# Causal attention inside a transformer block: where the masks are applied, how key tiles are paired, and how row sums are inverted

## Chip, cores and metric

One core of a Trainium2 chip runs the whole kernel in one launch. The metric is the device time of that launch in microseconds. Lower is better.

## What is computed

One adaLN transformer block in float32 on x of shape (2, 2048, 512): two sequences of 2048 tokens, width 512, 16 heads of 32. Cut to what matters here:

```python
mod = silu(condition) @ Wada + bada
sh_a, sc_a, gt_a, sh_m, sc_m, gt_m = split(mod, 6)
xm = layernorm(x, g1, be1) * (1 + sc_a) + sh_a
q, k, v = split(xm @ Wqkv)                      # 16 heads of 32
scores = where(causal, q @ k.T * 32 ** -0.5, -inf)
x = x + gt_a * (softmax(scores) @ v @ Wproj + bproj)
xm = layernorm(x, g2, be2) * (1 + sc_m) + sh_m
x = x + gt_m * (gelu(xm @ W1 + b1) @ W2 + b2)
```

## The kernel before

The program has four phases, one after the other: qkv, attention, projection, MLP. The change is in `phase_attention`, which runs 8 groups (2 sequences x 4 bundles of GH = 4 heads). `Plan` (a class that fixes the order of work for one group) cuts a group's causal triangle into 40 steps. A step is one key tile of 128 keys against one query chunk of 512 queries, for 4 heads. The chunks are taken from the last to the first (positions pos 0 to 3), with 16, 12, 8 and 4 key tiles. In the last four steps of each position the tile crosses the diagonal, and only the queries from `mid` on are computed: widths 512, 384, 256 and 128.

The softmax needs the maximum of every query row first. So there are two streams of work on TensorE:

* **The maxima of the next chunk** (`item`, tile `mx`, three PSUM banks). One item is a 128-query x up to 512-key tile of scores (L887), reduced along its row by VectorE (`tensor_reduce`, L800). A group has 160 such tiles (64 for pos 0, 48, 32, 16) and four small transposes of the collected maxima (`turn`, L879, L813, L815). 64 of the 160 tiles lie on the diagonal, in equal numbers of widths 128, 256, 384 and 512. TensorE may write a bank again only when VectorE has reduced the tile three items earlier (semaphore `mx_free`). `Plan.items_at` spreads the 164 items over the steps.
* **The steps themselves.** `scores` writes four tiles `st`, one per head (L907; the maximum is subtracted inside the matmul through two extra rows). ScalarE takes `Exp` of each into `prob` (L759). `product` multiplies the probabilities by v into `o_ps` (L925): four heads on four column groups of 32, which the trace shows as a run of 8. The row sums come by one of two ways: **direct**, a second run of ones x prob into `r_ps` (L930), or **pooled**, where GpSimd adds the whole `prob` tile of 2048 columns into `psum_k` (L740) and one run of ones x psum_k at the end (`total`, L942) adds it in.

The order on TensorE is written out by hand in `body`: scores of step s, then the product of step s - 1, with the items put between heads (`between`), between the product and the row sums, and behind them (`Plan.place`).

Causal masks are added on TensorE before: an extra matmul of a bfloat16 identity with a triangle of -1e30, into the last 128 columns of each diagonal tile (L890 for `mx`, L910 for `st`).

At the end of a position ScalarE copies `o_ps` and `r_ps` to SBUF (L768, L770), VectorE inverts the row sums in four pieces of 128 columns (`invert`, L824) and multiplies (`finish`, L830). SP stores `o_sb`. SP also sends the maxima through DRAM into the two extra rows of `q_st`.

## Time and profile before

| | |
|---|---|
| runs | 2533.92 us median of 3 (2533.89 to 2537.0) |
| profiled execution, first to last instruction (span) | 2531.2 us |
| around the span, against the median run | 2.7 us |
| busy in the span | PE 2367.6, PEld 1522.2, DVE 1370.5, ACT 907.9, POOL 731.3 us |
| attention, from the first product to the last | 391.6 to 1624.8 us |

The profile shows one execution. PE is TensorE's matmuls, PEld its weight loads, DVE VectorE, ACT ScalarE, POOL GpSimd, SP SyncE. A busy PE is no proof of a full PE, since matmuls are pipelined and a record is longer than the distance to the next one. Distances between starts are therefore read from the timeline where an engine's rate matters.

### The profile page before, as it was taken

The page shows a single profiled execution, that of the slowest core. Times are in us where ns is not written, and L with a number is a line of the kernel's source. Part 1 is how long each engine was busy: PE and PEld are TensorE (multiplying, and loading weights), DVE is VectorE, ACT ScalarE, POOL GpSimd, SP SyncE. Part 2 cuts the span into 40 slices and gives each one's busy share as a digit, 9 for nine tenths or more (in the row PEclk, how much of TensorE's full clock was granted, in tenths as well). Part 3 has the DMA queues.
Part 4 walks back from the last instruction along what each step waited for, and adds up shares of the span by engine and source line. Part 5 has one row for each costly group of instructions (what it writes and reads, how often), then busy time and mean ns, then how long its engine had stood idle before and what let it go on. Part 6 is the DMA issues. An engine that isn't in the chain of part 4 may idle for free. (4 is left out here: it accounts for less than half of the span.)

```text
span 2531.2 us, 38127 instructions
## 1 busy us (share of the span) xinstructions
PE 2367.6 (94%) x12615; PEld 1522.2 (60%) x12615; DVE 1370.5 (54%) x2406; ACT 907.9 (36%) x1772; POOL 731.3 (29%) x239
## 2 busy tenths in 40 slices
PE   6999958999999999999999999789599999999998
PEld 5888834444444444444444444467488888888887
DVE  6566455677777776776777773256622221221222
ACT  2111104454545545555454544311332222222221
POOL 1000025545554554555535554265000000000000
PEclk9999958999999999999999998789799999999999
DMA  5444464242242432515243211247521101110100
GB/s 183 167 182 174 158 158 102 55 96 63 64 98 56 105 69 53 109 40 125 49 91 79 60 35 47 87 176 244 171 84 50 50 1 49 50 50 0 50 33 17
DMA packets 129055, 223.34 MB, mean 88 GB/s; under 512 B 8448, under 2 KB 25912, under 8 KB 128828
## 3 DMA queue, kind: packets, MB, share of 16 engines
q1 hardware_dynamic: 105660, 175.18, 25.9%
q10 hardware_dynamic: 23232, 46.14, 5.0%
q8 instruction: 84, 1.38, 0.2%
q14 instruction: 79, 0.65, 0.1%
HBM read 145.26 MB, written 76.02 MB: 87 GB/s over the span
## 5 line engine op out<-in xcount | busy, mean ns | idle before, releaser
L800 DVE TENSOR_REDUCE part<-mx 128x1 f32<-128x512 f32 (+1 forms) x1249 | 690.2, 600 | 245.0 <-PE mx L890 127.8
L759 ACT ACTIVATE prob<-st 128x512 f32<-128x512 f32 (+3 forms) x1280 | 600.7, 538 | 579.0 <-PE st L907 357.7
L740 POOL TENSOR_TENSOR psum_k<-psum_k,prob 128x2048 f32<-128x2048 f32 (+3 forms) x136 | 519.0, 3817 | 242.3 <-ACT prob L759 238.4
L887 PE MATMUL mx<-k_st,qx_st 96*128 96x512 f32 (+1 forms) x1249 | 494.3, 422 | 41.2 <-DMA k_st<-qk_scratch 21.7
L907 PE MATMUL st<-q_st,k_st 98*128 98x512 f32 (+3 forms) x1280 | 471.4, 416 | 27.5 <-DMA q_st<-m_scratch 8.8
L887 PEld LDWEIGHTS mx<-k_st,qx_st 96*128 96x128 f32 x1249 | 241.3, 197 | 272.8 <-DVE part L800 223.9
L1442 DVE TENSOR_TENSOR m_g_lo<-m_g,m_g_hi 128x512 fp32r<-128x512 f32 x128 | 88.6, 692 | 511.8 <-ACT m_g_hi L1406 511.8
L907 PEld LDWEIGHTS st<-q_st,k_st 98*128 98x128 f32 x1280 | 243.0, 196 | 178.4 <-ACT prob L759 84.0
L925 PE MATMUL o_ps<-prob,v_sb 128*32 128x512 f32 (+3 forms) x2560 | 310.3, 557 | 0.0
L1402 ACT ACTIVATE m_g<-m_hid,vcol 128x512 f32<-128x512 f32 x128 | 88.3, 690 | 494.8 <-PE m_hid L1534 494.7
L740 POOL TENSOR_TENSOR psum_k<-prob 128x2048 f32<-128x2048 f32 x24 | 109.4, 4560 | 395.0 <-ACT prob L759 395.0
L1534 PE MATMUL m_hid<-m_xm_hi,w_hi 128*128 128x512 f32 x512 | 200.8, 392 | 16.3 <-DVEq L1471 10.4
L824 DVE RECIPROCAL o_raw<-o_raw 128x128 f32<-128x128 f32 x128 | 114.2, 926 | 166.5 <-ACT o_raw L770 165.2
L1534 PE MATMUL m_hid<-m_xm_hi,w_lo 128*128 128x512 f32 x512 | 199.7, 390 | 0.0
L1534 PE MATMUL m_hid<-m_xm_lo,w_hi 128*128 128x512 f32 x512 | 199.7, 390 | 0.0
L1512 PE MATMUL m_acc<-w_hi,m_g_hi 128*128 128x512 f32 x512 | 199.2, 389 | 0.0
L1512 PE MATMUL m_acc<-w_hi,m_g_lo 128*128 128x512 f32 x512 | 199.2, 389 | 0.0
L1512 PE MATMUL m_acc<-w_lo,m_g_hi 128*128 128x512 f32 x512 | 199.2, 389 | 0.0
L930 PE MATMUL r_ps<-prob,ones 128*32 128x512 f32 (+3 forms) x1088 | 125.1, 532 | 0.0
L1534 PEld LDWEIGHTS m_hid<-m_xm_hi,w_hi 128*128 128x128 f32 x512 | 96.5, 188 | 39.8 <-issue 19.9
L890 PE MATMUL mx<-mask_qk,ident_bf 128*128 128x128 bf16 x505 | 117.4, 236 | 0.0
L910 PE MATMUL st<-mask_kq,ident_bf 128*128 128x128 bf16 x512 | 116.9, 233 | 0.0
(160 smaller groups left out, 2667.7 us busy)
## 6 DMA issues: line engine op xcount, KB each, us to landing
qx_st<-qk_scratch SPq DMA_DIRECT2D x96, 256.0 KB, 4.5
k_st<-qk_scratch SPq DMA_DIRECT2D x96, 256.0 KB, 8.2
q_st<-qk_scratch SPq DMA_DIRECT2D x96, 256.0 KB
qk_scratch<-st_hi ACTq DMA_DIRECT2D x16, 1024.0 KB, 4.2
qk_scratch<-st_lo ACTq DMA_DIRECT2D x16, 1024.0 KB, 6.4
xs<-in_x_dram SPq DMA_DIRECT2D x8, 1024.0 KB, 5.3
v_scratch<-st_v ACTq DMA_DIRECT2D x8, 1024.0 KB, 4.3
v_sb<-v_scratch SPq DMA_DIRECT2D x8, 1024.0 KB, 14.6
```

The source lines that it names most:

```text
L740: nc.gpsimd.tensor_tensor(dst, src, prob[:, s % BUF, :, m:], ALU.add).then_inc(pool_added, 1)
L759: nc.scalar.activation(prob[:, s % BUF, h, m:], st[n % RING][:, m:], ACT.Exp, scale=SCALE).then_inc(exp_done, 1)
L800: nc.vector.tensor_reduce(part[:, pos % 2, h * TT + t, kc:kc + 1], bank[:, 0:w], AX.X, ALU.max).then_inc(mx_free, 1)
L824: nc.vector.reciprocal(r, r).then_inc(inverted, 1)
L887: ins = nc.tensor.matmul(out[:, 0:w], qx_st[0:ROWS, pos % 2, h, t * P:(t + 1) * P], k_st[0:ROWS, u, h, kc * CH:kc * CH + w], start=True, s ...
L890: ins = nc.tensor.matmul(out[:, w - P:w], K.ident_bf[:, :], K.mask_qk[:, :], start=False, stop=True)
L907: ins = nc.tensor.matmul(out[:, m:], k_st[0:MROWS, u, h, kt * P:(kt + 1) * P], q_st[0:MROWS, pos % 2, h, m:], start=True, stop=not masked)
L910: ins = nc.tensor.matmul(out[:, m:m + P], K.ident_bf[:, :], K.mask_kq[:, :], start=False, stop=True)
L925: ins = nc.tensor.matmul(o_ps[rows, m:], v_sb[:, u, kt, rows], prob[:, s % BUF, h, m:], start=(kt == 0), stop=end)
L930: ins = nc.tensor.matmul(r_ps[h * HD:(h + 1) * HD, m:], K.ones[:, 0:HD], prob[:, s % BUF, h, m:], start=(kt == 0), stop=end and pos == QC - 1)
L1512: ins = nc.tensor.matmul(acc[s][:, :], a, b, start=(j == 0 and k == 0), stop=(j == HT - 1 and k == 2))
L1534: ins = nc.tensor.matmul(hid[j % 4][:, :], a, b, start=(t == 0 and k == 0), stop=(t == KT - 1 and k == 2))
```

## The change

* **Masks.** The masking matmuls are gone. For the maxima, a diagonal tile is reduced by `tensor_tensor_reduce` on VectorE, which adds a mask row of 512 bfloat16 columns and takes the maximum. For the probabilities, GpSimd sets the triangle of 4 x 128 columns of each of the 16 diagonal steps of a group to zero after Exp (`affine_select`), and the product and the adds wait for it (`masked`).
* **Pairs.** Scores of two steps run one after the other, then the products of the two steps before, with nothing between. Items stand between the heads of the scores alone. `prob` has 5 buffers in place of 4.
* **Row sums.** A table `POOLED` says which key tiles GpSimd adds: 11, 8, 4 and 0 of the 16, 12, 8 and 4. That leaves 5, 4, 4 and 4 direct steps, 17 as before, of which 13 are diagonal ones. GpSimd has 20 adds a group, as before, now all of full width. `total` follows at once on the last product of a position.
* **Inversion.** VectorE transposes `r_ps` in 32 x 32 blocks, inverts 16 columns, transposes them back spread over 512, and multiplies. ScalarE's copy of `r_ps` is gone.
* The weights by which `Plan` spreads the items change, and `gate` is allocated after attention.

```diff
-    DIRECT = 3
+    POOLED = {3: (0, 1, 2, 4, 5, 6, 7, 9, 10, 11, 12), 2: (0, 1, 2, 4, 5, 6, 7, 8), 1: (0, 1, 2, 4), 0: ()}
...
-        weight = [self.width(s) + (P if self.steps[s][0] == 0 else 0) for s in range(self.NS)]
-        FROM, TO = 2, self.NS - 5
+        weight = [GH * max(self.width(s) / 2.4 + 13, 200) + 1.7 * self.width(s) for s in range(self.NS)]
+        FROM, TO = 2, self.NS - 6
...
-    BUF = 4
+    BUF = 5
...
+            def select(g, s):
+                n, m = L.selects.index(s), L.mid(s)
+                await_count(pool, held_pool, exp_done, exp_count(g, GH * (s + 1)))
+                tri = prob[:, s % BUF, :, m:m + P]
+                nc.gpsimd.affine_select(out=tri, in_=tri, compare_op=ALU.is_ge, fill=0.0, base=0,
+                                        pattern=[[0, GH], [1, P]], channel_multiplier=-1).then_inc(masked, 1)
...
             def body(g, u, more):
+                for s in range(L.NS):
+                    if s in L.selects:
+                        select(g, s)
+                    if s - 1 in L.adds:
+                        add(g, s - 1)
...
-                nc.scalar.activation(o_raw[:, pos % 2, 1, :], r_ps[:, :], ACT.Copy).then_inc(o_copied, 1)
...
-                dve.wait_ge(mx_ready, pre + 1)
-                nc.vector.tensor_reduce(part[:, pos % 2, h * TT + t, kc:kc + 1], bank[:, 0:w], AX.X, ALU.max).then_inc(mx_free, 1)
+                most = part[:, pos % 2, h * TT + t, kc:kc + 1]
+                if kc == L.order[pos]:
+                    await_count(dve, held_dve, mx_ready, pre + 1)
+                    nc.vector.tensor_tensor_reduce(spare[:, 0:w], bank[:, 0:w], K.mask_row[:, CH - w:], 1.0, LOWEST,
+                                                   ALU.add, ALU.max, most).then_inc(mx_free, 1)
+                else:
+                    dve.wait_ge(mx_ready, pre + 1)
+                    nc.vector.tensor_reduce(most, bank[:, 0:w], AX.X, ALU.max).then_inc(mx_free, 1)
...
-                nc.vector.reciprocal(r, r).then_inc(inverted, 1)
...
+            def normal(g, pos, part):
+                n = QC * g + pos
+                if part == 0:
+                    dve.wait_ge(r_ready, r_count(g, pos + 1))
+                    nc.vector.transpose(r_turn[:, :, :].rearrange("p b i -> p (b i)"), r_ps[:, :]).then_inc(r_taken, 1)
+                elif part == 1:
+                    dve.wait_ge(r_taken, n + 2)
+                    nc.vector.reciprocal(r_inv[:, :, :], r_turn[:, :, 0:1]).then_inc(r_inverted, 1)
...
+                elif part == 3:
+                    dve.wait_ge(r_spread, n + 1)
+                    dve.wait_ge(o_copied, n + 2)
+                    dve.wait_ge(o_sb_free, n + 1)
+                    nc.vector.tensor_tensor(o_sb[:, pos % 2, :], o_raw[:, pos % 2, :], r_wide[:, :],
+                                            ALU.mult).then_inc(o_done, 1)
...
-                if diagonal:
-                    ins = nc.tensor.matmul(out[:, w - P:w], K.ident_bf[:, :], K.mask_qk[:, :], start=False, stop=True)
...
-                    if masked:
-                        ins = nc.tensor.matmul(out[:, m:m + P], K.ident_bf[:, :], K.mask_kq[:, :], start=False, stop=True)
...
                 pe.wait_ge(exp_done, exp_count(g, GH * (s + 1)))
+                if L.diagonal(s):
+                    pe.wait_ge(masked, mask_count(g, L.selects.index(s) + 1))
...
-                    if s < L.NS:
-                        scores(g, u, s, between)
-                    elif more:
-                        scores(g + 1, 1 - u, 0)
-                    product(g, u, s - 1, between)
+                for b in range(1, L.NB + 1):
+                    for s in (2 * b, 2 * b + 1):
...
+                        if s < L.NS:
+                            scores(g, u, s, between)
+                        elif more:
+                            scores(g + 1, 1 - u, s - L.NS)
+                    for s in (2 * b - 2, 2 * b - 1):
+                        product(g, u, s)
```

How the order on the engines moves is shown at three places.

TensorE before, position 0, the products of steps 6 and 7. `mx` is a tile for the maxima, `st` a tile of scores, `o_ps` the product run, `r_ps` the row-sum run.

```order
837 L925 MATMUL o_ps<-prob,v_sb 32x512 x4
838 L876 REGISTER_ALU
839 L887 MATMUL mx<-k_st,qx_st 128x512
840 L930 MATMUL r_ps<-prob,ones 32x512 x4
841 L876 REGISTER_ALU
842 L887 MATMUL mx<-k_st,qx_st 128x512
843 L905 REGISTER_ALU
844 L907 MATMUL st<-q_st,k_st 128x512
```

TensorE of the change, the same position: the scores with their items end, then comes the product run of two steps (x8 is two runs of four), then the next scores.

```order
822 L938 MATMUL st<-q_st,k_st 128x512
823 L913 REGISTER_ALU
824 L923 MATMUL mx<-k_st,qx_st 128x512
825 L955 MATMUL o_ps<-prob,v_sb 32x512 x8
826 L937 REGISTER_ALU
827 L938 MATMUL st<-q_st,k_st 128x512
828 L913 REGISTER_ALU
829 L923 MATMUL mx<-k_st,qx_st 128x512
```

The `mx` matmuls that stood beside each product are between the scores now. Nothing that VectorE could reduce is issued while a product run lasts.

VectorE of the change, in position 1, where position 0's row sums are inverted. A diagonal tile is two instructions, both at L828: the one that writes `unused`, and one that writes `part`.

```order
493 L857 STREAM_TRANSPOSE r_turn<-r_ps 128x512
494 L51 REGISTER_ALU
495 L828 ISA unused,part<-mx,mask_row 128x512
496 L828 ISA part 128x1
497 L860 RECIPROCAL r_inv<-r_turn 128x16
498 L51 REGISTER_ALU
499 L828 ISA unused,part<-mx,mask_row 128x128
500 L828 ISA part 128x1
501 L863 STREAM_TRANSPOSE r_wide<-r_inv 128x512
502 L51 REGISTER_ALU
503 L828 ISA unused,part<-mx,mask_row 128x256
504 L828 ISA part 128x1
```

One part of the inversion is put in front of each reduction. Before, four reciprocals of 128 columns stood there, one in each of four steps.

## Rows read from the trace of the kernel before

**Rows 1.** Busy time by engine (PE, PEld, DVE, ACT, POOL), clock, DMA: attention alone.
```profile
391.60:1624.80 1233.20, 1186.60 (x7480) 572.65 (x7479) 843.08 (x1464) 627.96 (x1336) 628.48 (x160) 0.97 0.32 72
```

**Rows 2.** Waits between 420 and 1600 us: total, times, longest.
```profile
PEld mx L887 <- DVE part L800: 210.4, 297, 1.6
```

**Rows 3.** Timeline of PE: start us, us, op, count, idle before.
```profile
866.67 0.47 PE L887 MATMUL mx<-k_st,qx_st 96*128 96x512 f32 x1
866.99 0.23 PE L890 MATMUL mx<-mask_qk,ident_bf 128*128 128x128 bf16 x1
867.03 0.48 PE L907 MATMUL st<-q_st,k_st 98*128 98x512 f32 x1
...
868.54 0.40 PE L887 MATMUL mx<-k_st,qx_st 96*128 96x512 f32 x1
868.87 1.06 PE L925 MATMUL o_ps<-prob,v_sb 128*32 128x512 f32 x8
869.86 0.50 PE L887 MATMUL mx<-k_st,qx_st 96*128 96x512 f32 x1
870.29 1.06 PE L930 MATMUL r_ps<-prob,ones 128*32 128x512 f32 x8
871.29 0.50 PE L887 MATMUL mx<-k_st,qx_st 96*128 96x512 f32 x1
871.62 0.40 PE L907 MATMUL st<-q_st,k_st 98*128 98x512 f32 x1
871.86 0.40 PE L887 MATMUL mx<-k_st,qx_st 96*128 96x512 f32 x1
```

**Rows 4.** Timeline of PE where two runs follow each other directly.
```profile
994.34 1.07 PE L925 MATMUL o_ps<-prob,v_sb 128*32 128x512 f32 x8
995.22 1.04 PE L930 MATMUL r_ps<-prob,ones 128*32 128x512 f32 x8
996.19 0.38 PE L907 MATMUL st<-q_st,k_st 98*128 98x256 f32 x1
```

**Rows 5.** Groups by line and shape: busy us, mean ns; then idle before.
```profile
L890 PE MATMUL mx<-mask_qk,ident_bf 128*128 128x128 bf16 x505 | 117.4, 236 | 0.0
L910 PE MATMUL st<-mask_kq,ident_bf 128*128 128x128 bf16 x512 | 116.9, 233 | 0.0
```

**Rows 6.** Groups by line and shape: VectorE's reductions, reciprocals and one tiny operation.
```profile
L800 DVE TENSOR_REDUCE part<-mx 128x1 f32<-128x512 f32 x869 | 552.8, 681 | 162.0 <-PE mx L887 106.9 <-PE mx L890 51.1 <-DVE m_lo L815 1.7
L824 DVE RECIPROCAL o_raw<-o_raw 128x128 f32<-128x128 f32 x128 | 114.2, 926 | 166.5 <-ACT o_raw L770 165.2 <-DVE m_lo L815 1.1
...
L800 DVE TENSOR_REDUCE part<-mx 128x1 f32<-128x128 f32 x127 | 34.9, 275 | 53.2 <-PE mx L890 53.2
...
L99 DVE TENSOR_SCALAR tmp<-tmp 128x4 f32<-128x4 f32 x8 | 1.4, 169 | 0.3
```

**Rows 7.** Timeline of DVE: two full-width reductions in a row.
```profile
903.26 1.29 DVE L800 TENSOR_REDUCE part<-mx 128x1 f32<-128x512 f32 x2 [0.20 <-PE mx L887]
```

**Rows 8.** Timeline of POOL and DVE: the multiply that closes a position.
```profile
936.66 4.57 POOL L740 TENSOR_TENSOR psum_k<-psum_k,prob 128x2048 f32<-128x2048 f32 x1 [5.06 <-ACT prob L759]
...
939.52 2.26 DVE L830 TENSOR_TENSOR o_sb<-o_raw 128x512 f32<-128x512 f32 x1
```

**Rows 9.** Groups by line and shape: GpSimd's adds and a select.
```profile
L740 POOL TENSOR_TENSOR psum_k<-psum_k,prob 128x2048 f32<-128x2048 f32 x88 | 403.2, 4582 | 182.8 <-ACT prob L759 180.3
...
L209 POOL TENSOR_SCALAR_AFFINE_SELECT ident_bf<-ident_bf 128x128 bf16<-128x128 bf16 x1 | 0.3, 293 | 0.0
```

**Rows 10.** Timeline of the projection phase: DVE reads PSUM and SBUF while POOL adds.
```profile
1780.13 4.99 POOL L1109 TENSOR_TENSOR p_xs<-p_gated,p_xs 128x512 f32<-128x512 f32 x4 [11.14 <-DVE p_gated L1191]
...
1782.79 0.69 DVE L1191 TENSOR_TENSOR p_gated<-p_acc,gate 128x512 f32<-128x512 f32 x1 [1.61 <-PE p_acc L1254]
```

**Rows 11.** Timeline of PE at the start of a group.
```profile
1007.22 2.01 PE L907 MATMUL st<-q_st,k_st 98*128 98x512 f32 x4 [3.92 <-issue]
1009.16 1.93 PE L925 MATMUL o_ps<-prob,v_sb 128*32 128x512 f32 x8
```

More of the change, by code:

```diff
@@ L480, in direct, with first_direct, diagonal @@
         pos, kt = self.steps[s]
-        return pos == QC - 1 or kt % self.DIRECT == 0
+        return kt not in self.POOLED[self.order[pos]]
+    def first_direct(self, s):
+        pos, _ = self.steps[s]
+        return self.direct(s) and not any(self.direct(r) for r in range(s) if self.steps[r][0] == pos)
+    def diagonal(self, s):
+        pos, kt = self.steps[s]
+        return kt >= self.order[pos] * TT
     def mid(self, s):
@@ L500, in stream, with own_until @@
         return [i for i in self.items_at[s] if more or self.group(0, i) == 0]
+    def own_until(self):
+        return max(s for s in range(self.NS) if self.stream(s, False))
     def group(self, g, i):
@@ L520, in phase_attention @@
     ROWS, MROWS = 3 * HD, 3 * HD + 2
-    BUF = 4
+    BUF = 5
     RING = 3
-    INV = 4
+    SQ = 32
     M0, M1 = M_GTA, M_GTM + KT
-    MOD_AT, LOAD_AT = (25, 28, 34, 37), (28, 31)
     EACH = 6
+    first = L.own_until() + 1
+    MOD_AT = tuple(first + 3 * n for n in range(4))
+    LOAD_AT = (MOD_AT[0] + 3, MOD_AT[1] + 3)
     MROW = GH * TT
@@ new lines, in body @@
+            def body(g, u, more):
+                for b in range(1, L.NB + 1):
+                    items = L.stream(2 * b, more) + L.stream(2 * b + 1, more)
+                    ending = [p for p in range(QC - 1) if L.last_block[p] + 2 == b]
+                    for k in range(max(len(items), 6 if ending else 0)):
+                        if ending and k >= 2:
+                            normal(g, ending[0], k - 2)
+                        if k < len(items):
+                            i = items[k]
+                            item(L.group(g, i), item_count(g, i), L.items[i], mx[i % RING], unused[:, i % RING, :])
+                for k in range(4):
+                    normal(g, QC - 1, k)
@@ L927, in product, with total @@
                 if L.direct(s):
-                    between(GH)
+                    opens = L.first_direct(s)
+                    if opens:
+                        pe.wait_ge(r_taken, QC * g + pos + 1)
                     for h in range(GH):
                         ins = nc.tensor.matmul(r_ps[h * HD:(h + 1) * HD, m:], K.ones[:, 0:HD], prob[:, s % BUF, h, m:],
-                                               start=(kt == 0), stop=end and pos == QC - 1)
+                                               start=opens, stop=end and pos == QC - 1)
                 ins.then_inc(pv_done, 1)
-                between(GH + 1 if L.direct(s) else GH)
-                if end and pos == QC - 1:
+                if end:
+                    total(g, s, pos)
+            def total(g, s, pos):
+                if pos == QC - 1:
                     pe.wait_ge(pv_done, pv_count(g, s + 1))
-                    pe.sem_inc(o_ready, 1)
-            def total(g, pos):
-                n = sum(s <= L.last[pos] for s in L.adds)
+                    pe.sem_inc(r_ready, 1)
+                    return
+                n = sum(r <= s for r in L.adds)
                 pe.wait_ge(pool_added, add_count(g, n))
```

188 lines of the change are left out of this document (88 added, 100 removed).

## Prediction

> **What bounds the kernel now.** I first read the busy times of attention alone, from the first product to the last: 1233.2 us for 8 groups, so 154 us a group [rows 1]. PE is busy 1186.6 us of it, DVE 843.1, ACT 628.0 and POOL 628.5. The reader should see that PE is the bound and that DVE, the next one, has 68% of its time filled. The phases before and after attention are not touched, so the whole change is decided here. Then I read the waits: PEld waits 210.4 us, 297 times, for DVE to reduce a tile (`mx_free`) [rows 2]. These waits are short (1.6 us at most) and mostly lie under a running matmul, but they say that VectorE's three banks are the second limit, close behind. The timeline of PE gives the rates: two full-width plain matmuls start 0.24 us apart (871.62 to 871.86), while a record is 0.40 long [rows 3]. DVE starts full-width reductions 0.61 us apart (1.29 less the 0.68 of the second) [rows 6, 7]. So one tile and the `st` beside it cost PE 0.48 us and DVE 0.61 us. Where items crowd, DVE is the slower of the two.
>
> **The change on TensorE.** *Masks.* With its mask a full tile takes 0.36 us to the next start (866.67 to 867.03), without 0.24: 0.12 saved [rows 3]. The lower bound is 0.04, the distance from the mask to the next start. There are 1017 masks, 127 a group [rows 5]: 5 to 15 us a group. *Pairs.* Entering a run costs 0.33 in place of 0.24 (868.54 to 868.87), leaving it 0.99 in place of 0.88 where the next run follows directly, and the matmul behind takes 0.33 in place of 0.24 (871.29 to 871.62) [rows 3, 4]. That is 0.3 us for each time PE changes over. A group has 40 product runs and some 9 row-sum runs that stand apart; 20 pairs remain: 29 x 0.3 = 9 us. *Row sums.* The direct steps of a group have 7168 columns now and 5632 after, 3 runs of 512 less: 3 x 0.88 = 3 us. Together TensorE sheds 17 to 27 us of 154.
>
> **VectorE.** Four positions x four reciprocals x 0.86 us go (0.93 busy, less an overlap of 0.07 as in the reductions) [rows 6]: 14 us a group. What comes: two transposes of 512 columns, taken as 0.6 us each like a reduction, and a reciprocal of 16 columns, 0.2: 6 us in four positions. And 64 tiles become masked reductions of two instructions. The first I take like a plain reduction of its width. The second is not in this trace. Its bounds are nothing and 0.17 us, the duration of an operation on 128x4 [rows 6]; I take 0.10, nearer to that row since it has to follow its partner: 6 us. So VectorE's work hardly falls, 14 less against 12 more.
>
> **What the pairing does to VectorE is the step on which all turns.** Before, tiles stood beside and between the runs, so DVE always had something to reduce. Now it gets none during two to four runs (1.9 to 3.6 us), only the three tiles in the banks. For a pair with n items the stretch of scores lasts the longer of
>
> * PE: (8 + n) x 0.24
> * DVE: 0.9 + (n - 3) x d, since item n can be issued when item n - 3 is reduced; 0.9 is the way from the first score to the first reduction and from the last release to the last matmul (two plain starts and a matmul's record of 0.40).
>
> d is the mean distance of reductions: 0.61 at 512, 0.20 at 128 (0.275 less the same overlap), on the mean of a group's 96 full and 64 diagonal tiles 0.525 plus 0.4 x 0.10 = 0.565 [rows 6, 7]. The plan of the changed kernel gives the pairs 15, 9, 9, 10, 12, 11, 6, 11, 14, 14, 11, 8, 6, 9, 10, 8, 1, 0, 0, 0 items. From nine on DVE is the longer term, for 12 of the 20. Summed: 7.7 + 2 x 7.1 + 6.0 + 3 x 5.4 + 2 x 4.9 + 3 x 4.3 + 2 x 3.8 + 2 x 3.4, and some 10 for the four pairs without tiles: 91 us. The runs: 19456 product columns are 38 x 0.88, row sums 11 x 0.88, three totals 2.6, 20 changes of 0.3: 52 us. The four transposes of maxima, each with a chain of small operations on DVE, cost about 1 us each: 4. The wait that PE shows at the start of every second group (3.92 us, and a product run of 1.93 us behind it in place of 1.06) stays [rows 11]: 2 to 3.
>
> *The multiply.* One more wait grows. The multiply that closes a position took 2.26 us where GpSimd was adding and ended 0.55 us after that add did; undisturbed it would be as long as other passes of 512 columns, 0.69 [rows 8, 10]. It reads two tiles in SBUF. GpSimd's adds grow from 78 us a group to 20 x 4.58 = 92, plus 16 selects [rows 9], in a shorter or equal time, so the multiply meets an add in most positions and waits half of it, 2.3 us. Three of four positions have tiles queued behind it on DVE, and PE behind those. With the transposes (1.5 us) and 0.6 for itself: some 4 us each, 12 in a group.
>
> Sum of a group: 91 + 52 + 4 + 2.5 + 12 = 161.5 against 154: **7 us more**, in 7 groups 49. The last group has no tiles of a following one after half its steps, so it is bound by PE there and keeps about half of what PE sheds, 10 us. The opening 16 diagonal tiles add 2. I round the sum of +41 down to +36, since of the waits counted here some fall together. The profiled execution's 2531 becomes 2567; the median of the runs is 2.7 us above its span, so **2570 us**.
>
> The page "VectorE: DVE Perf Modes" of the Trainium skill, section "The TRN2 errata — SBUF-src ops pay a fixed extra latency per instruction", gives a PSUM-to-SBUF operation 120 cycles plus its columns at 0.96 GHz. At 512 columns that is an estimate of 0.66 us, where the trace's reductions start 0.61 apart; by the page's rate the crowded pairs would be some 5 us a group longer still, about 2610 us. The measured distance decides.
>
> *Selects on GpSimd.* One select on 128 columns took 0.29 us [rows 9]; on 4 x 128, between 0.3 and four of them, 1.2 us. Sixteen make at most 19 us a group, with the adds 111 of 160. The product waits for the select, but a pair later, some 6 us after Exp. That covers one add of 4.58 and a select. I cost it at nothing; without the cover it is the rival below. ScalarE loses a copy and bounds nothing.
>
> **The rivals.**
>
> 1. *The masked reductions and the multiply are cheap, and PE's gain comes through* (faster). If the second instruction is free, d is 0.525, and 99 crowded intervals give back 4 us; if the multiply seldom meets an add, 7 more. A group is then 150.5, and the time is 2534 - 25 - 10, about 2500. It decides where d plus the closing work falls below what PE sheds. For it: TensorE's saving is certain, and half of the multiplies of before were undisturbed. Against it: GpSimd's adds fill more of the group. Chance 0.24.
> 2. *Both sides cancel* within 5 us: 0.08.
> 3. *GpSimd is late with a select* (slower). It is in order, so the first diagonal steps of a position have their selects behind adds of 4.58 us. If each of two such places in a group lets PE wait for a whole add, that is 9 us a group on top, 2640. It decides if a select takes 2 us or more. Chance 0.09.
> 4. *The masked reduction meets GpSimd's adds as the multiply does*, since its mask row is in SBUF. Each of 64 tiles would wait 0.6 x 2.3 us, some 90 us a group, over 3200 us. The trace speaks against it: a pass that read one tile in PSUM and one in SBUF took 0.69 us in the middle of four adds of GpSimd [rows 10]. Chance 0.02.
> 5. *The clock.* PE's idle pieces grow. After the 3.92 us of idleness a product run took 1.93 us in place of 1.06 [rows 11], which is the lower of the two clock levels. If longer waits in crowded pairs bring that back, each costs a few us. Chance 0.02, beyond 2600.
> 6. My forecast, VectorE's rate in crowded pairs, slower by 10 to 75 us: 0.55; its own range is 2545 to 2610.
>
> **How the numbers follow.** About 0.2% (5 us) is what a measurement of this kernel can tell from no change. Faster is rival 1, 0.24; same is rival 2, 0.08; slower the rest, 0.68. The range leaves out the fast end of rival 1 (below 2505) and rivals 4 and 5: 2505 to 2635.
>
> **What would show it.** In the changed profile: PE's busy time in attention falls by over 100 us while the span of attention does not; waits of PE for DVE's reductions grow to several times 210 us and are longest in the pairs with 14 and 15 items; DVE idles in the product runs; the multiply lasts over 2 us on the mean; no wait on a select shows. The forecast is wrong if PE's waits for DVE stay near 200 us, if the accumulator's instruction is free, or if PE waits for GpSimd.

## The result, and the profile after

| | before | after |
|---|---|---|
| runs | 2533.9 us median of 4 (2528.32 to 2537.0) | 2592.22 us median of 4 (2584.19 to 2600.81) |
| profiled execution, span | 2531.2 us | 2599.1 us |
| attention, first to last product | 1233.2 us | 1297.5 us |
| one group, mean of the first seven | 153.1 us | 162.9 us |
| mean granted TensorE clock over the whole span | 0.961 | 0.910 |

The change makes the kernel slower: after / before is 1.0237, interval 1.0205 to 1.0269, which is 60 us. In the profiled executions attention accounts for 64 us of a difference of 68. The first product starts 7 us later (398.5 against 391.6), and what follows attention is 3 us shorter.

The busy times and the clock strip of the page, after:

```profile
PE 2380.6 (92%) x11591; PEld 1535.2 (59%) x11591; DVE 1311.7 (50%) x2886; ACT 923.9 (36%) x1740; POOL 912.2 (35%) x363
...
PEclk9999958888988989889898888679799999999999
```

Busy times by engine (PE, PEld, DVE, ACT, POOL), clock and DMA of attention after. Below it, after the dots, is the same for the stretch from 400 to 1600 us, by which the experiments are compared:

```profile
398.50:1696.00 1297.50, 1191.65 (x6451) 580.32 (x6454) 779.99 (x1903) 638.99 (x1295) 801.63 (x287) 0.87 0.30 67
...
400.00:1600.00 1200.00, 1098.54 (x5935) 532.80 (x5928) 767.34 (x1865) 600.89 (x1208) 751.70 (x265) 0.89 0.31 68
```

and that stretch before:

```profile
400.00:1600.00 1200.00, 1153.96 (x7266) 553.47 (x7264) 835.48 (x1452) 616.38 (x1310) 623.79 (x159) 0.98 0.32 72
```

The reader should see three things against [rows 1]. TensorE has a thousand matmuls fewer (x7480 to x6451) and is busy as long as before (1186.6 to 1191.7). DVE is busy 63 us less, though it reduces as many tiles. And the granted clock of attention fell from 0.97 to 0.87. Summed from the trace's record of the clock, attention ran 329 us at half clock (1.2 GHz in place of 2.4), before 66. A record at half clock is longer (a score matmul 0.63 us in place of 0.40, shown below), so PE's busy time hides that it has less to do.

Waits from 420 to 1600 us, after (total, times, longest):

```profile
PEld mx L923 <- DVE part L832: 160.2, 426, 3.3
PEld mx L923 <- DVE part L828: 84.6, 163, 4.0
...
PE mx L923 <- DVE part L828: 36.2, 39, 3.6
...
PE mx L923 <- DVE part L832: 30.3, 42, 2.8
```

Where one row said 210.4 us, 297 times, 1.6 at most [rows 2], the waits for VectorE are now 245 us on PEld, 589 times, up to 4.0, and 67 more on PE itself (17 before). Together that is 311 us against 227: more, but not several times as much.

Groups by line and shape, after: the new and the changed operations of DVE and POOL (busy us, mean ns; then idle before).

```profile
L828 DVE CUSTOM_DVE_ANT_0 unused<-mx,mask_row 128x512 bf16<-128x512 f32 x125 | 85.9, 687 | 70.3 <-PE mx L923 66.3 <-DVE m_lo L847 2.9 <-issue 0.2
...
L869 DVE TENSOR_TENSOR o_sb<-o_raw,r_wide 128x512 f32<-128x512 f32 x32 | 56.2, 1755 | 0.6
...
L828 DVE DVE_READ_ACCUMULATOR2_ANT part<- 128x1 f32 x512 | 42.5, 83 | 0.0
...
L857 DVE STREAM_TRANSPOSE r_turn<-r_ps 128x512 f32<-128x512 f32 x32 | 22.9, 715 | 197.8 <-PE r_ps L976 139.6 <-PEq L971 56.6 <-DVE m_lo L847 1.5
L863 DVE STREAM_TRANSPOSE r_wide<-r_inv 128x512 f32<-128x512 f32 x32 | 22.6, 707 | 0.6
...
L758 POOL TENSOR_TENSOR psum_k<-psum_k,prob 128x2048 f32<-128x2048 f32 x136 | 621.8, 4572 | 183.7 <-ACT prob L784 178.7 <-POOL psum_k L758 0.4
...
L742 POOL TENSOR_SCALAR_AFFINE_SELECT prob<-prob 128x512 f32<-128x512 f32 x128 | 81.6, 647 | 206.5 <-ACT prob L784 206.5
```

A masked reduction of 512 columns takes 687 ns, like a plain one (681), and its second instruction 83 ns. A select takes 0.65 us. The multiply takes 1.76 us on the mean; before it was this row:

```profile
L830 DVE TENSOR_TENSOR o_sb<-o_raw 128x512 f32<-128x512 f32 x32 | 49.3, 1542 | 0.6
```

**A pair at full clock.** TensorE between 1059 and 1064 us (start us, us, op, count): the product run of two steps, a row-sum run, the next scores.

```profile
1060.23 1.92 PE L955 MATMUL o_ps<-prob,v_sb 128*32 128x512 f32 x16
1061.97 1.04 PE L962 MATMUL r_ps<-prob,ones 128*32 128x512 f32 x8
1062.95 0.50 PE L938 MATMUL st<-q_st,k_st 98*128 98x512 f32 x1
```

DVE beside it (idle before in brackets):

```profile
1060.86 0.68 DVE L832 TENSOR_REDUCE part<-mx 128x1 f32<-128x512 f32 x1
1063.72 5.47 DVE L832 TENSOR_REDUCE part<-mx 128x1 f32<-128x512 f32 x9 [2.18 <-PE mx L923]
1070.51 4.88 DVE L832 TENSOR_REDUCE part<-mx 128x1 f32<-128x512 f32 x8 [1.32 <-PE mx L923]
```

DVE runs dry in each product run (2.18 and 1.32 us), then reduces without a gap at 5.47 / 9 = 0.61 us a tile, and TensorE follows at that rate.

**Pairs in one group** (1211.6 to 1374.9 us). Stretches of scores by busy time of each engine and clock: 9 and 10 items at full clock, then the two pairs of 14 and the one of 15 items.

```profile
1223.13:1228.07 4.94, 4.94 (x22) 2.74 (x18) 4.17 (x7) 4.27 (x8) 4.86 (x2) 1.00 0.98 220
1229.92:1235.46 5.54, 5.44 (x23) 2.92 (x19) 4.77 (x8) 4.29 (x8) 5.46 (x2) 1.00 0.00 0
1268.43:1277.71 9.28, 7.09 (x27) 4.51 (x23) 7.77 (x30) 4.21 (x8) 6.99 (x2) 0.78 0.70 152
1280.89:1289.93 9.04, 7.79 (x26) 5.16 (x22) 6.33 (x27) 4.50 (x8) 3.31 (x1) 0.66 0.41 91
1363.05:1374.83 11.78, 8.29 (x24) 5.76 (x24) 10.10 (x32) 4.96 (x9) 8.17 (x2) 0.62 0.37 92
```

In the last three the clock is at its lower level for part of the time (0.78, 0.66, 0.62 on the mean). The crowd is not the only thing that is special about them. One more stretch of this group is as long, and it has ten items only (1320.79 to 1331.15 us, where the pair of ten above took 5.54). TensorE first, then VectorE:

```profile
1329.57 0.79 PE L923 MATMUL mx<-k_st,qx_st 96*128 96x512 f32 x1 [2.83 <-DVE part L832]
...
1331.15 3.64 PE L955 MATMUL o_ps<-prob,v_sb 128*32 128x512 f32 x16
...
1325.87 3.04 DVE L869 TENSOR_TENSOR o_sb<-o_raw,r_wide 128x512 f32<-128x512 f32 x1
```

VectorE is in the closing multiply of a position, TensorE waits 2.83 us for the reduction behind it, the clock falls (at 1328.2), and the product run that follows lasts 3.64 us where it lasted 1.92. The pair of 15 is the same: TensorE waits 3.31 us behind the multiply of the group's last position (2.69 us). The two pairs of 14 have a wait of 1.09 us, behind the maxima's chain and a transpose of the row sums, and one of 1.16 us, for the collected maxima. These four waits of over 1 us come back in nearly every group, and four of the five falls of the clock in this group begin during one of them or within 2 us behind it.

What the lower level does to TensorE is in its timeline in the fourth of them:

```profile
1285.20 0.63 PE L938 MATMUL st<-q_st,k_st 98*128 98x512 f32 x1
1285.63 0.63 PE L923 MATMUL mx<-k_st,qx_st 96*128 96x128 f32 x2
1286.06 0.63 PE L938 MATMUL st<-q_st,k_st 98*128 98x512 f32 x1
```

A score matmul of 512 columns now takes 0.43 us to the next start, where it took 0.24 [rows 3]. The Trainium skill, page "TensorE: Matmul & The Clock Gate", section "Part 1: The HAM clock gate (the "warmup" mystery)", gives 426.7 ns at the lower level; the trace agrees. At that pace a tile and its `st` take TensorE 0.86 us, longer than the 0.61 that VectorE needs, so the pair that waited for VectorE a moment before is now bound by TensorE.

### The profile page after: what moved, and what is told of

Its sections match the earlier page's. It is cut to its first block and busy times, and to the rows that moved or that the text cites. A ratio compares the mean times of both kernels' runs of the same rounds, so it can differ in the third digit from the quotient of the medians.

```text
span 2599.1 us, 37450 instructions
## 1 busy us (share of the span) xinstructions
PE 2380.6 (92%) x11591; PEld 1535.2 (59%) x11591; DVE 1311.7 (50%) x2886; ACT 923.9 (36%) x1740; POOL 912.2 (35%) x363
## 5 line engine op out<-in xcount | busy, mean ns | idle before, releaser
L784 ACT ACTIVATE prob<-st 128x512 f32<-128x512 f32 (+3 forms) x1280 | 629.3, 537 | 624.9 <-PE st L938 612.3
L758 POOL TENSOR_TENSOR psum_k<-psum_k,prob 128x2048 f32<-128x2048 f32 x136 | 621.8, 4572 | 183.7 <-ACT prob L784 178.7
L923 PE MATMUL mx<-k_st,qx_st 96*128 96x512 f32 (+1 forms) x1249 | 540.5, 459 | 99.4 <-DVE part L828 36.9
L938 PE MATMUL st<-q_st,k_st 98*128 98x512 f32 (+3 forms) x1280 | 516.4, 426 | 29.5 <-ACT prob L784 9.0
L832 DVE TENSOR_REDUCE part<-mx 128x1 f32<-128x512 f32 x744 | 456.3, 681 | 130.9 <-PE mx L923 130.9
L923 PEld LDWEIGHTS mx<-k_st,qx_st 96*128 96x128 f32 x1249 | 265.9, 215 | 313.4 <-DVE part L832 170.6
L955 PE MATMUL o_ps<-prob,v_sb 128*32 128x512 f32 (+3 forms) x2560 | 337.5, 639 | 0.0
L828 DVE CUSTOM_DVE_ANT_0 unused<-mx,mask_row 128x512 bf16<-128x512 f32 (+2 forms) x505 | 228.7, 486 | 205.6 <-PE mx L923 180.3
L955 PEld LDWEIGHTS o_ps<-prob,v_sb 128*32 128x32 f32 x2560 | 73.8, 121 | 153.3 <-issue 94.1
L742 POOL TENSOR_SCALAR_AFFINE_SELECT prob<-prob 128x512 f32<-128x512 f32 x128 | 81.6, 647 | 206.5 <-ACT prob L784 206.5
```

What stands on the lines that cost most here:

```text
L742: nc.gpsimd.affine_select(out=tri, in_=tri, compare_op=ALU.is_ge, fill=0.0, base=0, pattern=[[0, GH], [1, P]], channel_multiplier=-1).then ...
L758: nc.gpsimd.tensor_tensor(dst, src, prob[:, s % BUF, :, :], ALU.add).then_inc(pool_added, 1)
L784: nc.scalar.activation(prob[:, s % BUF, h, m:], st[n % RING][:, m:], ACT.Exp, scale=SCALE).then_inc(exp_done, 1)
L828: nc.vector.tensor_tensor_reduce(spare[:, 0:w], bank[:, 0:w], K.mask_row[:, CH - w:], 1.0, LOWEST, ALU.add, ALU.max, most).then_inc(mx_fre ...
L832: nc.vector.tensor_reduce(most, bank[:, 0:w], AX.X, ALU.max).then_inc(mx_free, 1)
L923: nc.tensor.matmul(out[:, 0:w], qx_st[0:ROWS, pos % 2, h, t * P:(t + 1) * P], k_st[0:ROWS, u, h, kc * CH:kc * CH + w], start=True, stop=Tr ...
```

## The experiments

Ratios are against before on the same chip, with their 95% interval; in brackets is the difference that they make of 2534 us. "Half clock" is the time at the lower clock within attention, in the one execution that was profiled.

| | ratio | half clock, us |
|---|---|---|
| after | 1.0237 [1.0205, 1.0269] (+60) | 329 |
| e1 masks moved alone | 1.0188 [1.0149, 1.0227] (+48) | 236 |
| e8 as e1, masks kept on TensorE too | 1.0102 [1.0078, 1.0126] (+26) | 100 |
| e9 before, no causal masks at all | 0.98 [0.9773, 0.9828] (-51) | 103 |
| e2 inversion alone | 0.9959 [0.994, 0.9977] (-10) | 85 |
| e3 after, masks on TensorE | 1.0268 [1.0227, 1.031] (+68) | 257 |
| e12 after, pairing undone | 1.0241 [1.0207, 1.0275] (+61) | 239 |
| e10 after, both undone | 0.9908 [0.9876, 0.9939] (-23) | 83 |
| e11 as e10, row sums in PSUM | 0.9891 [0.9846, 0.9936] (-28) | 95 |
| e4 after, product runs filled | 1.0164 [1.0125, 1.0202] (+42) | 275 |
| e5 after, multiply reads PSUM | 1.0166 [1.0123, 1.0208] (+42) | 311 |
| e6 after, plain reductions | 1.0104 [1.0078, 1.0129] (+26) | 315 |
| e7 after, matmuls doubled | 1.0218 [1.0193, 1.0243] (+55) | 214 |

### One part of the change alone

**e1**, the masks moved and nothing else:

```diff
-                nc.vector.tensor_reduce(part[:, pos % 2, h * TT + t, kc:kc + 1], bank[:, 0:w], AX.X, ALU.max).then_inc(mx_free, 1)
+                if kc == L.order[pos]:
+                    nc.vector.tensor_tensor_reduce(spare[:, 0:w], bank[:, 0:w], K.mask_row[:, CH - w:], 1.0, LOWEST,
+                                                   ALU.add, ALU.max, most).then_inc(mx_free, 1)
...
-                    ins = nc.tensor.matmul(out[:, w - P:w], K.ident_bf[:, :], K.mask_qk[:, :], start=False, stop=True)
-                        ins = nc.tensor.matmul(out[:, m:m + P], K.ident_bf[:, :], K.mask_kq[:, :], start=False, stop=True)
...
+                if L.diagonal(s):
+                    pe.wait_ge(masked, mask_count(g, L.selects.index(s) + 1))
```

> The kernel before with the masks alone moved: the 512 diagonal tiles of the maxima are reduced with a mask row on VectorE, the triangles of the probabilities are zeroed on GpSimd; single steps, items beside the products, old inversion, old choice of pooled tiles. If VectorE starved by the pairing is the cause (my theory), the tiles come evenly here, TensorE keeps part of the 5 to 15 us a group that it sheds, and the kernel is between 2500 and 2534 us. If the masked reductions themselves are the cause (two instructions, 0.08 us for the second in the changed kernel's trace), they cost here too and the time is 2540 or more. If the clock is what the mask matmuls held up, the granted clock falls from 0.96 here as well.

Measured: 2584.68 us, +48, against my theory, which had 2534 at most. The masks alone cost nearly as much as the whole change. From 400 to 1600 us:

```profile
400.00:1600.00 1200.00, 1098.12 (x6099) 509.12 (x6091) 840.36 (x1930) 594.60 (x1272) 684.45 (x274) 0.93 0.31 69
```

A wait that is new:

```profile
PE o_ps L953 <- POOL prob L744: 18.0, 19, 1.9
```

In single steps the product comes one step after Exp, and TensorE waits for some selects (18 us on PE, the same again on PEld). The granted clock falls to 0.93.

**e2**, the new inversion alone, on ScalarE's copy of the row sums:

```diff
-                nc.vector.reciprocal(r, r).then_inc(inverted, 1)
+                if j == 0:
+                    nc.vector.transpose(r_turn[:, :, :].rearrange("p b i -> p (b i)"), r).then_inc(inverted, 1)
+                elif j == 1:
+                    nc.vector.reciprocal(r_inv[:, :, :], r_turn[:, :, 0:1]).then_inc(inverted, 1)
```

> The kernel before with the inversion alone changed: two 32x32 transposes and a reciprocal of 16 columns in place of four reciprocals of 128, from the SBUF copy of the row sums. VectorE loses some 8 us a group. My theory: tensorE is the bound before, so little comes, 2515 to 2534 us. Rival (VectorE's queue is what ends the waits already before): 2490 or less.

Measured: 2526.57 us, -10. From 400 to 1600 us DVE is busy 763 us where it was 835, so it gets back 73 us, and 10 reach the end: in the order of before, little of VectorE's time is on the path.

### Undoing one part of the two that cost

**e3**, the masks back on TensorE, the pairs kept:

```diff
-                if L.diagonal(s):
-                    pe.wait_ge(masked, mask_count(g, L.selects.index(s) + 1))
...
+                    if L.diagonal(s):
+                        ins = nc.tensor.matmul(st[n % RING][:, m:m + P], K.ident_bf[:, :], K.mask_kq[:, :], start=False, stop=True)
```

> The changed kernel with the masks back on TensorE: pairs, new inversion and new pooled tiles stay. If pairing starves VectorE, this is still clearly slower than before, 2545 to 2580, though a little faster than the changed kernel, since the masked reductions cost VectorE 0.08 us each and TensorE has room to spare. If the masked reductions are the cause, it comes back to 2534 or below. If TensorE's idle pieces lower the clock, the granted clock is between 0.91 and 0.96, since the masks fill some of them.

Measured: 2603.42 us, +68, where I had expected 2580 at most. The interval overlaps that of after: it gives nothing back.

**e12**, the pairing undone (order of TensorE, ScalarE and VectorE, and Plan's weights), the masks left where the change puts them:

```diff
-                for b in range(1, L.NB + 1):
-                    for s in (2 * b, 2 * b + 1):
+                for s in range(1, L.NS + 1):
...
-                    for s in (2 * b - 2, 2 * b - 1):
-                        product(g, u, s)
+                    product(g, u, s - 1, between)
```

> The changed kernel with the pairing alone undone: single steps with the items beside the products, the spread of items of before; masks on VectorE and GpSimd, new inversion and new pooled tiles stay. If the pairing costs what the run with TensorE's masks in pairs suggests, some 60 us or more less the changes of run that come back (9 us a group at most), this is 2540 to 2570, faster than 2592. If the masks' move is all of the loss, it stays at 2580 or above. A product here waits for a select that was issued one step earlier, so waits on GpSimd appear (36 us in the run with the masks alone moved).

Measured: 2595.85 us, +61: nothing back either, where I had expected 20 us or more. One wait says why the pairs are not to be judged alone:

```profile
PE o_ps L952 <- POOL prob L743: 60.1, 36, 2.6
PEld o_ps L952 <- POOL prob L743: 56.0, 29, 2.8
```

In single steps, with GpSimd's adds on the key tiles of the new table, TensorE waits 60 us for selects (and its weight loads 56). In the change these waits are 1.1 us. The pairing hides the selects and costs as much elsewhere. "Pairing" stands here and below for the pairs together with their spread of the items; the two were not run apart.

**e10**, both undone: the edits of e3 and of e12 together. What stays of the change is the inversion, the table of pooled key tiles and five buffers.

> The changed kernel with single steps as before (items beside the products, the spread of items of before) and the masks back on TensorE: of the change the new inversion, the new pooled tiles and the fifth buffer stay. Pairs plus masks then account for all of the loss. TensorE saves 3 us of row-sum runs a group and VectorE some 8 us: I expect 2490 to 2520, faster than before. If the loss came from GpSimd's full-width adds, it is 2540 or more.

Measured: 2511.1 us, -23: faster than before.

```profile
400.00:1600.00 1200.00, 1152.88 (x7445) 575.86 (x7441) 769.41 (x1422) 610.02 (x1296) 722.38 (x159) 0.97 0.32 72
```

**e11**, e10 with the inverted row sums spread into the bank they came from, so that the multiply reads one tile in PSUM:

```diff
-                    nc.vector.tensor_tensor(o_sb[:, pos % 2, :], o_raw[:, pos % 2, :], r_wide[:, :],
+                    nc.vector.tensor_tensor(o_sb[:, pos % 2, :], o_raw[:, pos % 2, :], r_ps[:, :],
```

> The run before this one, with the inverted row sums spread back into their PSUM bank, so that the closing multiply reads one tile in PSUM and one in SBUF. The multiply should fall to 0.7 us. Since TensorE is the bound in this order, I expect 0 to 20 us on top. The rival is that the next position's first direct row sums then wait for the multiply and nothing comes.

Measured: 2509.2 us, -28. The intervals of e10 and e11 overlap; both are faster than either kernel.

The four corners, with the new inversion in all of them:

| | masks on TensorE | masks moved |
|---|---|---|
| single steps | -23 (e10) | +61 (e12) |
| pairs | +68 (e3) | +60 (after) |

Moving the masks costs 84 us in single steps and nothing in pairs; pairing costs 91 us with the masks on TensorE and nothing without. Each of the two brings the whole loss; together they bring it once.

### The clock

**e8**, e1 with the masking matmuls left in as well, so that TensorE has its old work on top of every new wait (the edit against e1):

```diff
+                if kc == L.order[pos]:
+                    ins = nc.tensor.matmul(out[:, w - P:w], K.ident_bf[:, :], K.mask_qk[:, :], start=False, stop=True)
...
+                    if L.diagonal(s):
+                        ins = nc.tensor.matmul(out[:, m:m + P], K.ident_bf[:, :], K.mask_kq[:, :], start=False, stop=True)
```

> The run with the masks alone moved (2585 us, 236 us of attention at half clock) with the masking matmuls of TensorE kept as well, so that every mask is applied twice. The result is the same; TensorE has all the work of the kernel before, VectorE and GpSimd that of the masks moved. If the clock made the masks' move slow, TensorE's extra work brings the half-clock time near 66 us and the kernel back to 2535 to 2555, faster with more work. If masked reductions on VectorE or the waits on GpSimd's selects made it slow, it is 2585 or more.

Measured: 2565.68 us, +26, so 22 us faster than e1 although it does 1017 matmuls more; the intervals do not touch (the two ran on different chips, each beside before). The two profiled executions lie only 10 us apart, at 2582.2 and 2572.1 us of span.

```profile
400.00:1600.00 1200.00, 1129.41 (x7097) 540.18 (x7097) 847.55 (x1936) 602.33 (x1278) 686.75 (x276) 0.98 0.32 69
```

The clock is back at 0.98. At one clock, work put into the order of TensorE can make nothing behind it start earlier, as long as no operation's own length changes. The one operation here whose length depends on its neighbours is the closing multiply, and it takes 1.75 us on the mean in e1 and 1.74 in e8. So the gain has to come from the clock.

The product and row-sum runs show it directly. Summed over attention, from the first matmul of a run to the next score or `mx` matmul, in us:

| | runs | of it at half clock | runs less half of that |
|---|---|---|---|
| before | 433.3 | 30.3 | 418 |
| e1 | 474.6 | 114.7 | 417 |
| e8 | 442.5 | 51.0 | 417 |
| e10 | 409.9 | 34.0 | 393 |
| e12 | 446.0 | 106.5 | 393 |
| after | 426.8 | 144.1 | 355 |
| e3 | 402.6 | 95.1 | 355 |
| e7, below | 390.8 | 69.9 | 356 |

The last column comes out the same wherever the order of the runs is the same, so a run at half clock takes twice its time, with nothing to cover it. From e1 to e8 the runs lose 32 us, and the stretches between them, where the extra matmuls are, gain 22; that is the 10 us between the profiled executions. In e1 then some 22 us of the 48 are the lower clock, net of what the extra matmuls cost in e8. The other 26 are what is left for the masked reductions and the waits for selects; those two were not told apart.

**e9**, before with the two masking matmuls deleted. Its output lacks the causal masks, so it is a measurement and no kernel to use:

```diff
-                    ins = nc.tensor.matmul(out[:, w - P:w], K.ident_bf[:, :], K.mask_qk[:, :], start=False, stop=True)
...
-                        ins = nc.tensor.matmul(out[:, m:m + P], K.ident_bf[:, :], K.mask_kq[:, :], start=False, stop=True)
```

> The kernel before with the masking matmuls left out and nothing in their place: the causal masks are missing. TensorE sheds 1017 matmuls, 40 to 120 us by my term, and no other engine gets work. If TensorE's own clock gives nothing back, the time is 2410 to 2495. If the shed work lowers the clock, as in the run with the masks alone moved (236 us at half clock against 66), the half-clock time rises to 150 us or more and the time is above 2495.

Measured: 2487.15 us, -51, half clock 103 us, where 150 or more would have shown that the shed work alone lowers the clock.

```profile
400.00:1600.00 1200.00, 1115.12 (x6449) 526.72 (x6449) 843.44 (x1480) 614.95 (x1330) 625.37 (x159) 0.95 0.33 73
```

The same matmuls taken away are worth 51 us here and cost 22 between e8 and e1. What differs is whether TensorE can use the time: in e9 VectorE has no more to do than before, in e1 it has. TensorE's idle time in attention is 44 us before, 73 in e9 and 103 in e1, and the half clock goes the same way (66, 103, 236).

**e7**, after with zero to nine score matmuls of each crowded pair run twice, as many as would fill the idle pieces:

```diff
+                    for _ in range(((s % 2) * GH + h + 1) * extra // 8 - ((s % 2) * GH + h) * extra // 8):
+                        nc.tensor.matmul(st[n % RING][:, m:], k_st[0:MROWS, u, h, kt * P:(kt + 1) * P],
+                                         q_st[0:MROWS, pos % 2, h, m:], start=True, stop=True)
```

> The changed kernel with some matmuls of scores issued twice into the same bank, in the pairs of nine items and more, in the number that my rule for a pair leaves TensorE idle (0 to 9 of 0.24 us). The result is the same. Theory of the clock: TensorE's idle pieces are filled, the time at half clock in attention (329 us in the changed kernel, 66 before) falls, and the kernel is faster than 2592 although it does more. Theory of VectorE's rate alone: the time is the same, or up to 20 us more, whatever the clock does.

Measured: 2594.54 us, +55, not to be told from after. The gain that the theory of the clock asked for did not come; the time is the one that VectorE's rate alone would give. But half-clock time fell, from 329 to 214 us.

```profile
400.00:1600.00 1200.00, 1113.41 (x6338) 597.75 (x6336) 777.17 (x1893) 606.97 (x1214) 756.43 (x266) 0.93 0.31 69
```

In the profiled executions the runs are 36 us shorter than in after, by the clock alone (the table above), and the stretches of scores, where the filler stands, 24 us longer. The filler raises the clock and eats most of what that brings.

**The clock's price in the change itself** has a lower bound from the same table. The order of the change saves TensorE 63 us in the runs (418 to 355), and the clock takes 57 of them back (half of 144.1 less 30.3). The stretches of scores, with 184.9 us at half clock against 36.1, come on top, by an amount that VectorE's part in them hides. It is a gross price: how much of the 57 us the kernel would get, were the clock full, stays open, since VectorE also reduces while a run lasts. The four executions of the change point the same way. The shortest has a span of 2582.5 us at a mean clock of 0.915, the longest 2599.1 at 0.910: some 29 us more at half clock (an estimate from these numbers) go with 17 us more of time.

### VectorE in the change

**e6**, the diagonal tiles of the maxima reduced like the others:

```diff
-                if kc == L.order[pos]:
+                if False:
```

> The changed kernel with plain reductions of the diagonal tiles: the mask is left out of the maxima, so a row's maximum may be over masked keys too. It has the same number of tiles and no second instruction. If VectorE's work per tile is what counts, 64 x 0.08 us a group go: 15 to 35 us gained. If the clock and the shape of the pairs rule, less than 8 us.

Measured: 2568.47 us, +26, so 34 less than after. It takes away 512 x 0.083 = 42.5 us of VectorE's time and half clock stays at 315 us: here VectorE's instructions are on the path, four fifths of them. (A row's maximum may be over masked keys in this run.)

**e4**, two items of each pair with eight or more put between and behind the product runs:

```diff
-                    for s in (2 * b - 2, 2 * b - 1):
-                        product(g, u, s)
+                    product(g, u, 2 * b - 2)
+                    for i in kept[:1]:
+                        stream_item(g, u, i)
+                    product(g, u, 2 * b - 1)
+                    for i in kept[1:]:
+                        stream_item(g, u, i)
```

> The changed kernel with two of the items of each pair of eight or more taken out of the scores and put one between the two product runs and one behind them. TensorE pays up to 0.3 us for each change of run, some 12 a group. My theory: VectorE gets tiles while the products run, the waits for its reductions fall from 314 us by a third, and the kernel gains 15 to 40 us on the changed one's 2592. If VectorE's idle time in the runs is not the cause, it is the same or slower (2592 to 2620).

Measured: 2578.72 us, +42, so 18 less than after. That VectorE runs dry in the product runs is shown to cost, though giving it two tiles there returns only a third of the loss.

**e5**, the multiply reads `o_ps` in PSUM, and ScalarE's copy of it is gone:

```diff
-                    nc.vector.tensor_tensor(o_sb[:, pos % 2, :], o_raw[:, pos % 2, :], r_wide[:, :],
+                    nc.vector.tensor_tensor(o_sb[:, pos % 2, :], o_ps[:, :], r_wide[:, :],
```

> The changed kernel with the closing multiply reading the products straight from PSUM; ScalarE's copy of them is gone and TensorE's next position waits for the multiply. The multiply then reads one tile in SBUF and one in PSUM. In the changed kernel's trace it takes 1.85 us on the mean against 0.69 undisturbed. My term for it: the multiply falls to 0.7 us and the kernel gains some 8 us a position that has tiles queued, in all 10 to 50 us on 2592. If the wait for GpSimd's adds is nothing that counts, it is within 8 us of 2592.

Measured: 2584.83 us, +42, again 18 less, though its interval just overlaps that of after, so the size is rough. The multiply is now

```profile
L858 DVE TENSOR_TENSOR o_sb<-o_ps,r_wide 128x512 f32<-128x512 f32 x32 | 22.0, 687 | 0.6
```

0.69 us in place of 1.76, in the middle of the same adds. In the change one of the long ones was this, DVE first, then GpSimd:

```profile
1163.38 3.04 DVE L869 TENSOR_TENSOR o_sb<-o_raw,r_wide 128x512 f32<-128x512 f32 x1
...
1161.34 4.53 POOL L758 TENSOR_TENSOR psum_k<-psum_k,prob 128x2048 f32<-128x2048 f32 x1 [0.26 <-ACT prob L784]
```

The add ends at 1165.87 and the multiply 0.55 us behind it, the same distance as in [rows 8]. The Trainium skill, page "SBUF — State Buffer", section "SBUF: two separate sides", says that a VectorE operation with two inputs in SBUF and a GpSimd operation that reads SBUF exclude each other for a whole instruction, and names no such case for an input in PSUM. By it the multiply should fall to its own length once one input is in PSUM, and the measured 687 ns agree with it.

## Why the prediction was right, and where it was not

The time was forecast as 2570 us and is 2592: slower, within the range of 2505 to 2635 and within the forecast's own of 2545 to 2610. The sum came close for one group, and that is partly luck: two of its parts were off and made up for each other.

**A group.** Forecast 161.5 us, measured 162.9. In the group from 1211.6 us on, the 20 stretches of scores sum to 110.7 us, where 91 for the pairs, 4 for the maxima, 12 for the closing work and 2.5 for the group's start made 109.5. The runs take the other 52.6 us (forecast 52). But 16.6 us of the runs and 23.8 us of the stretches were at half clock, which the sum held at nothing. At full clock the runs would be 44 us. The forecast's 52 had room for the rest: it took 19456 product columns, where a group has 17408 (28 runs of 512 columns and four each of 384, 256 and 128, so 34 x 0.88 in place of 38 x 0.88, 3.5 us less), and it added 6 us for changes, of which the timeline shows the larger part outside the runs (1059.80 to 1060.23, 0.19 us over the plain distance).

**The pair rule held near full clock, away from the closing work.** 10 items: 5.54 us measured, 4.85 by the rule; 12: 6.41 and 6.0; 11: 5.18 to 6.03 and 5.4; 9: 4.93 to 5.34 and 4.3. It is up to 1 us short. The pair of ten with the closing multiply took 10.35. VectorE's distance in such a pair was 0.61 us as read from [rows 7]. e6 and e4 confirm the two halves of the argument: VectorE's instructions are on the path, and its idleness in the runs costs.

**The clock is the step that failed.** I had it as rival 5, at 0.02 and "a few us" each, beyond 2600, and not in the sum. It came in every group, and the time stayed below 2600 all the same: attention ran 329 us at half clock against 66. I had priced the clock by one product run behind one idle piece [rows 11] and did not ask what the waits do to it that I had forecast myself. Those waits are four in a group, of 1.0 to 3.6 us, and the two longest are behind the closing multiply, which the sum had as a wait of VectorE and not as a fall of the clock. What it costs is shown in single steps (e8 against e1, 22 us net) and, gross, in the runs of the change (57 us); its net share in the change is open (e7). The pairs of 14 and 15 items took 9.28, 9.04 and 11.78 us where the rule had 7.1, 7.1 and 7.7. These 8 us are not the clock's alone, since the closing work and the maxima's chain, which the sum had apart, are in them too.

**PE's busy time** was to fall by over 100 us and rose by 5, for that reason: the matmul count fell as said, and the records grew.

**The closing work was set too high**, and this too made room for the clock in the sum. The waits of over 1 us behind it in that group are 1.09, 2.83 and 3.31 us, 7 in place of 12. That three of four positions have tiles queued behind it was right. The multiply measured 1.76 us on the mean, not 2.9, and was already 1.54 before. Its contact with GpSimd, with ScalarE's copy, is worth some 18 us in all (e5), 2 us a group. The transposes measured 0.71 us (forecast 0.6), the reciprocal 0.25 (0.2), the accumulator's instruction 0.083 (0.10).

**Masks on TensorE**: forecast 5 to 15 us a group, measured 51 / 8 = 6.4 (e9), near the lower bound. By the distance to the next start in [rows 3] it would be 15. In e9 TensorE's idle time in attention is 29 us longer than before and its half-clock time 37, so part of what the masks gave up went there; that this is all of the rest is argued, not shown.

**Selects costed at nothing** is right in the change (0.65 us each, waits of 1.1 us in all). But the prediction gave them no part in the pairing: without it they cost TensorE 60 us of waits (e12). I had priced the masks as a gain and the pairs as a loss. The corners show that each costs some 85 us alone and that neither is cheaper undone. Why two losses of that size add up to one is not explained. One piece is shown: with the pairs the selects are hidden (60 us of waits in e12, 1.1 in the change). The rest was not measured apart.

**Ends.** I compared with 154 us, the mean of all eight groups. The last one was 161.3 us long, the other seven 153.1, so the loss in seven groups was 7 x 9.8 = 69 us, not 49. The last group gained 4 us, not 10. Summed, attention is 64 us longer where the prediction had 41. The opening is 7 us later, not 2: the runs with pairs start attention at 396 to 401 us and those without at 388 to 392, so it comes with the pairs, whose first product has more scores ahead of it.

**The signs.** Of what I said would show it, three came: attention is longer, VectorE idles in the product runs, and no wait on a select shows. Three did not. PE's busy time did not fall. The multiply lasts 1.76 us on the mean, not over 2. And the waits for VectorE's reductions grew from 227 us to 311 on PE and its weight loads together, not to several times 210; nor are the longest all in the pairs of 14 and 15, since one of 2.83 us is in a pair of ten. By the words of the prediction waits that stay near 200 us would have spoken against it, and 245 on the weight loads is not far from that. VectorE's part is shown better by e6 than by this sign.

Of the rivals, rival 1 (cheap masked reductions and multiply) fell: they are cheaper than I took them, and it stayed 60 us slow. Rivals 3 and 4 did not occur: no wait on a select, and the masked reduction, which reads a mask row in SBUF beside a tile in PSUM, takes 687 ns amid the adds.

## What to carry to other kernels

When a change takes work from the engine that bounds, ask first whether the next engine leaves it able to use the time: if not, the gain turns into waits, and here the clock fell with them, so that less work took longer. Read the granted clock beside the busy time: here the busy time stayed while the count of matmuls fell by a thousand. Look for the few long waits that come back in every group before the many short ones. And where a change has several parts, run the corners: here undoing either part gave nothing, and undoing both gave a kernel faster than the one before.

## What the hardware did that I had not expected

* TensorE with 1017 matmuls more (e8 against e1) was 22 us faster, with the granted clock from 400 to 1600 us at 0.98 in place of 0.93.
* The same matmuls removed where VectorE had not been loaded (e9) went with a clock of 0.95 and brought 51 us.
* The product and row-sum runs of attention, less half of their time at half clock, come to 417 or 418 us in before, e1 and e8 and to 355 or 356 in after, e3 and e7, whatever the clock was: nothing covers a run at half clock.
* A masked reduction of VectorE costs its plain length plus 83 ns: 687 ns at 512 columns, 284 at 128, with a bfloat16 output that nobody reads.
* A multiply with both inputs in SBUF takes 1.76 us on the mean beside GpSimd's adds, with one input in PSUM 0.69 us.
